# Layer 2 mixture of experts in a four-layer decoder: weighted rows scattered behind each expert, loaded in order, and the last expert's rows added by one product

## What is computed

```python
logits = xf @ Wr.T
topk_vals, topk_idx = jax.lax.top_k(logits, TOP_K)             # TOP_K = 2
w_flat = softmax(topk_vals).reshape(-1)
sort_idx = jnp.argsort(topk_idx.reshape(-1))                   # 1600 (token, expert) rows, sorted by expert
rev = sort_idx // TOP_K
chunks = xf[rev].reshape(Ne, S // Ne, Ds)                      # 200 rows for each expert, in order
h = gelu(einsum('ecd,edf->ecf', chunks, W1), approximate=False)
eo = einsum('ecf,efd->ecd', h, W2).reshape(S, Ds)
out = zeros((N, Ds)).at[rev].add(eo * w_flat[sort_idx][:, None])
```

## Time and profile before

| | us |
|---|---|
| three runs | 1495.36, 1498.70, 1505.01 |
| median | 1498.7 |
| the profiled execution's own time | 1495.78 |
| its span, first to last instruction | 1494.0 |
| PE busy, share of the span | 91% |
| granted TensorE clock, mean | 0.954 |

### The profile page before, as it was taken

How to read it: one execution, slowest core, us unless ns; L and a number is a source line. 1 busy time by engine, 2 the same in 40 slices (tenths; PEclk the granted TensorE clock), 3 DMA queues, 4 the chain that set the end, 5 groups by cost and what they waited for, 6 DMA issues and landing times. The chain is left out here.

```text
span 1494.0 us, 31527 instructions
## 1 busy us (share of the span) xinstructions
PE 1353.9 (91%) x12488; PEld 1054.5 (71%) x12488; DVE 769.4 (52%) x1733; ACT 646.7 (43%) x1683; POOL 194.9 (13%) x200
## 2 busy tenths in 40 slices
PE   7999899989989899899999889989957896899887
PEld 6776668866557588778999765669955675578632
DVE  3666677655556677520000477501127485566765
ACT  3444226633366366344444246432225674256300
POOL 3000250000024200050110420040042000300000
PEclk9999999989999999899999989989988997999999
DMA  6000331011301200366996100545211000700100
GB/s 217 1 1 1 68 65 22 4 44 43 80 8 21 46 11 4 130 210 244 343 342 261 49 22 1 227 166 202 74 52 40 1 2 1 118 5 4 68 1 22
DMA packets 43943, 120.19 MB, mean 80 GB/s; under 512 B 11931, under 2 KB 28440, under 8 KB 38412
## 3 DMA queue, kind: packets, MB, share of 16 engines
q1 hardware_dynamic: 33048, 62.04, 14.4%
q0 software_dynamic: 7616, 53.12, 10.3%
q10 hardware_dynamic: 3136, 3.03, 0.7%
HBM read 95.78 MB, written 11.00 MB: 71 GB/s over the span
## 5 line engine op out<-in xcount | busy, mean ns | idle before, releaser
L826 PE MATMUL wide<-early_kt,early_q 32*100 32x361 f32 x512 | 95.4, 485 | 2.8 <-PEq L66 1.6
L2555 ACT ACTIVATE l1f_hidden<-wide,l1f_pack 128x128 f32<-128x128 f32 x160 | 58.8, 368 | 78.0 <-PE wide L2494 68.1
L2677 DVE TENSOR_TENSOR l1f_out<-summed,l1f_pack 128x256 f32<-128x256 f32 x20 | 8.5, 425 | 152.8 <-PE summed L2502 152.8
L2494 PEld LDWEIGHTS wide<-l1f_rt,l1f_pack 128*128 128x128 f32 x640 | 74.5, 192 | 1.7 <-issue 0.8
L2494 PE MATMUL wide<-l1f_rt,l1f_pack 128*128 128x128 f32 x640 | 74.8, 275 | 0.6 <-ACT l1f_rt L2545 0.6
L113 PE MATMUL summed<-ident 128*128 128x128 f32 x302 | 44.4, 314 | 33.2 <-PEq L66 33.2
L2502 PE MATMUL summed<-l1f_pack,l1f_hidden 128*128 128x256 f32 x320 | 72.4, 379 | 0.0
L113 PEld LDWEIGHTS summed<-ident 128*128 128x128 f32 x302 | 42.2, 226 | 38.9 <-issue 38.9
L2502 PEld LDWEIGHTS summed<-l1f_pack,l1f_hidden 128*128 128x128 f32 x320 | 59.2, 190 | 7.2
L3688 PE MATMUL wide<-l3f_we,l3f_xt 128*100 128x512 f32 x128 | 59.6, 620 | 1.2 <-DVE l3f_acc L3756 1.2
L1220 DVE TENSOR_REDUCE l3x_mx<-wide 100x2 f32<-100x722 f32 x64 | 55.3, 904 | 3.2 <-PE wide L826 3.0
(11 more groups left out here) (605 smaller groups left out, 3369.8 us busy)
## 6 DMA issues: line engine op xcount, KB each, us to landing
l2f_w<-l2f_w_dram SPq DMA_DIRECT2D x16, 1024.0 KB, 11.5
ctxt<-ctxt_dram SPq DMA_DIRECT2D x4, 1083.0 KB, 17.1
early_kt<-soon_kd SPq DMA_DIRECT2D x32, 90.8 KB, 3.3
l1f_sorted_x<-l1f_zeros SPq DMA_DIRECT2D x4, 640.0 KB
l1f_rows<-l1f_sorted_x SPq DMA_DIRECT2D x20, 128.0 KB, 7.5
l1f_sorted_y<-l1f_out ACTq DMA_DIRECT2D x20, 128.0 KB, 9.4
l0f_w<-l0f_w_dram SPq DMA_DIRECT2D x18, 128.0 KB, 2.1
l1f_shared<-l1f_shared_dram SPq DMA_DIRECT2D x1, 2180.0 KB, 9.0
```

Source lines behind the costliest of these rows:

```text
L826: pe.matmul(wide[0:S, i, 0:SKV], q4[R * i:R * (i + 1), g % 2, b, g // 2, :], kt[R * i:R * (i + 1), g % 2, b, g // 2, 0:SKV], start=True, s ...
L2494: last = pe.matmul(wide[:, f % 4, 0:P], w1_of(w, k, f), rt[:, n % 2, k, :], start=k == 0, stop=k == KC - 1)
L2555: act.activation(hidden[:, f, 0:P], wide[:, f % 4, 0:P], ACT.Gelu, bias=b1_of(pack[:, n % SLOTS, :], f)).then_inc(sem["h_ready"], 1)
L2677: dve.tensor_tensor(out[:, n % 2], summed[:, n % 2, 0:E], b2_of(pack[:, n % SLOTS, :]), ALU.add).then_inc(sem["y_ready"], 1)
```

## The change

Rows now carry three more numbers (`ROW = E + 3`): the weight of the token for this expert, the slot in which the result is to lie, and the token's number. Two new inputs, `l2f_tags` and `l2f_numbers`, are loaded for it. `xn` holds two copies of the normalised tokens, one for each choice, and the weights are made early: ACT begins with the Exp table, takes the exponential ahead of the unit copies and then loads the Gelu table. Behind each of the experts 0 to 6, DVE scales `out` by the rows' weights and POOL scatters it to `token_y`, each row to its token's slot, with two indirect DMAs. Zeros are scattered to the slots of the last expert. SP then loads `token_y` in order, in four parts, and DVE adds them to x. The last expert's rows don't go through DRAM: `spot`, made of `numbers` on DVE, holds the weight where row and token meet, and PE multiplies it with `out` (`unsort`), in eight pieces that DVE adds to x. The units ahead of the experts are 28 (`AHEAD = 6`); `rest[0]` and `turn_out(6)` stand between the experts 6 and 7, and ACT makes the copies of expert 7. The statistics of layer 3's norm are taken at the end of `l2_ffn`, piece by piece behind the additions, and `keep_busy` in `l3_attn` goes from 18 to 4.

```diff
-    AHEAD = 4
+    AHEAD = 6
+    ROW = E + 3
+    PARTS = 4
+    FIN = NE - 1
...
+        tags, numbers = sb("tags", [S, TOP, B, 2]), sb("numbers", [S, B * S])
+        pairs = [(wr[:], dram["l2f_wr"]), (t.iota[:], dram["iota8"]), (before[:], dram["before"]), (tags[:], dram["l2f_tags"]),
+                 (numbers[:], dram["l2f_numbers"].partition_broadcast(S))]
         n_loaded = 16 * len(pairs)
-        xn = sb("xn", [S, B, E])
+        tokens = sb("tokens", [S, TOP * B * ROW])
+        xn = tokens[:].rearrange("s (k b e) -> s k b e", k=TOP, b=B)
+        back = tokens[:, 0:TOP * B * E].rearrange("s (n e) -> s n e", e=E)
...
+        rows = sb("rows", [S, SLOTS, RT, ROW])
+        about, target = sb("about", [S, NE, RT, 3]), sb("target", [S, NE * RT], U32)
+        spot = sb("spot", [S, RT, B * S])
+        none = sb("none", [S, E])
...
+        token_y = nc.dram_tensor("token_y", (ROWS, E), F32).ap()
...
                     if e + SLOTS < NE:
                         sp.wait_ge(sem["rt_psum"], e + 1)
+                        sp.wait_ge(sem["about_ready"], e + 1)
                         load_rows(e + SLOTS)
                         sp.wait_ge(sem["y_psum"], e + 1)
                         load_expert(e + SLOTS)
-                    sp.wait_ge(sem["y_ready"], e + 1)
-                    sp.dma_start(sorted_y.rearrange("(e r s) d -> e s r d", r=RT, s=S)[e], out[:, e % 2]).then_inc(stored[e % 2], 16)
+                sp.wait_ge(sem["none_stored"], 16 * RT)
+                for slot in range(2):
+                    sp.wait_ge(stored[slot], 16 * RT * ((FIN + 1 - slot) // 2))
+                for n in range(PARTS):
+                    some = slice(n * TOP * B // PARTS, (n + 1) * TOP * B // PARTS)
+                    sp.dma_start(back[:, some], token_y.rearrange("(n s) d -> s n d", s=S)[:, some]).then_inc(gathered[n], 16)
...
+                pool.memset(none[:], 0.0)
+                pool.drain()
                 pool.wait_ge(sem["place_ready"], 1)
                 for b in range(B):
                     for k in range(TOP):
                         pool.indirect_dma_start(out=sorted_x, out_offset=bass.IndirectOffsetOnAxis(ap=placei[:, k * B + b:k * B + b + 1], axis=0),
-                                                in_=xn[:, b, :], in_offset=None).then_inc(sem["scattered"], 16)
-                for slot in range(2):
-                    pool.wait_ge(stored[slot], 16 * NE // 2)
-                for b in range(B):
-                    for k in range(TOP):
-                        pool.indirect_dma_start(out=back[:, k * B + b, :], out_offset=None, in_=sorted_y,
-                                                in_offset=bass.IndirectOffsetOnAxis(ap=placei[:, k * B + b:k * B + b + 1], axis=0)
-                                                ).then_inc(gathered[k * B + b], 16)
+                                                in_=xn[:, k, b, :], in_offset=None).then_inc(sem["scattered"], 16)
+
+                def scatter(e, source, done):
+                    for c in range(RT):
+                        pool.indirect_dma_start(out=token_y, out_offset=bass.IndirectOffsetOnAxis(ap=target[:, e * RT + c:e * RT + c + 1], axis=0),
+                                                in_=source(c), in_offset=None).then_inc(done, 16)
+
+                for e in range(FIN):
+                    pool.wait_ge(sem["y_ready"], e + 1)
+                    scatter(e, lambda c: out[:, e % 2, c, :], stored[e % 2])
+                pool.wait_ge(sem["about_ready"], NE)
+                scatter(FIN, lambda c: none[:], sem["none_stored"])
...
+                def unsort(b):
+                    bank = (turned, summed)[b % 4 // 2][0:S, b % 2, b // 4 * E:(b // 4 + 1) * E]
+                    if b >= 4:
+                        pe.wait_ge(sem["added"], b - 3)
+                    for c in range(RT):
+                        last = pe.matmul(bank, spot[:, c, b * S:(b + 1) * S], out[:, FIN % 2, c, :], start=c == 0, stop=c == RT - 1)
+                    last.then_inc(sem["back_psum"], 1)
+
+                rest = order[2 * (B + AHEAD):]
...
+                        if e == FIN and f == unit[rest[0]] % RING:
+                            pe.wait_ge(unit_free[f], unit[rest[0]] // RING + 1)
                         for k in range(KC):
                             last = pe.matmul(wide[:, f % 4, 0:CR], w1[:, e % SLOTS, k, f * P:(f + 1) * P], rt[:, e % 2, k, :], start=k == 0, stop=k == KC - 1)
                         last.then_inc(sem["h_psum"], 1)
-                    if e >= 1:
+                    if 1 <= e < FIN:
                         turn_out(e - 1)
                     if e + 1 < NE:
                         turn(e + 1)
                     weigh(e)
-                rest = order[2 * (B + AHEAD):]
-                project(rest[0])
-                turn_out(NE - 1)
-                for what in rest[1:]:
+                    if e == FIN - 1:
+                        project(rest[0])
+                        turn_out(e)
+                project(rest[1])
+                turn_out(FIN)
+                project(rest[2])
+                pe.wait_ge(sem["spot_ready"], RT)
+                pe.wait_ge(sem["y_ready"], NE)
+                for b in range(B):
+                    unsort(b)
+                for what in rest[3:]:
                     project(what)
...
-                act.preload_act_table(ACT.Gelu)
+                act.preload_act_table(ACT.Exp)
...
+                act.wait_ge(sem["gap_ready"], 1)
+                act.activation(t.exp[:], t.gap[:], ACT.Exp).then_inc(sem["exp_ready"], 1)
+                act.preload_act_table(ACT.Gelu)
...
-                act.wait_ge(sem["gap_ready"], 1)
-                act.activation(t.exp[:], t.gap[:], ACT.Exp).then_inc(sem["exp_ready"], 1)
-                for what in order[2 * (B + AHEAD):]:
+                    if e == FIN - 1:
+                        copy_unit(rest[0])
+                act.wait_ge(sem["y_psum"], NE)
+                act.activation(yt[:, FIN % 2], summed[:, 0, 0:KC * CR].rearrange("p (m s) -> p m s", m=KC), ACT.Copy).then_inc(sem["yt_ready"], 1)
+                act.wait_ge(stored[FIN % 2], 16 * RT * (FIN // 2))
+                act.wait_ge(sem["o_psum"], NE)
+                act.activation(out[:, FIN % 2], summed[0:S, 1, :].rearrange("s (c e) -> s c e", c=RT), ACT.Copy).then_inc(sem["y_ready"], 1)
+                act.preload_act_table(ACT.Sqrt)
+                for what in rest[1:]:
                     copy_unit(what)
+                act.wait_ge(sem["var_ready"], 2)
+                act.activation(net.std[:], net.std[:], ACT.Sqrt).then_inc(sem["std_ready"], 1)
...
+                    normalise(dve, net, xn[:, 0, b, 0:E], b).then_inc(sem["xn_ready"], 1)
+                for b in range(B):
+                    normalise(dve, net, xn[:, 1, b, 0:E], b)
...
+                dve.tensor_copy(xn[:, :, :, E + 1:ROW], tags[:])
...
+                dve.wait_ge(sem["exp_ready"], 1)
+                dve.tensor_scalar(t.den[:], t.exp[:], 1.0, None, ALU.add)
+                dve.drain()
+                dve.reciprocal(xn[:, 0, :, E:E + 1], t.den[:])
+                dve.drain()
+                dve.tensor_tensor(xn[:, 1, :, E:E + 1], t.exp[:], xn[:, 0, :, E:E + 1], ALU.mult)
...
                 dve.tensor_copy(placei[:], place[:].rearrange("s k b -> s (k b)")).then_inc(sem["place_ready"], 1)
-                for e in range(NE):
+
+                def learn(e):
+                    dve.wait_ge(r_loaded[e % SLOTS], 16 * (e // SLOTS + 1))
+                    dve.tensor_copy(about[:, e], rows[:, e % SLOTS, :, E:ROW])
+                    dve.drain()
+                    dve.tensor_copy(target[:, e * RT:(e + 1) * RT].unsqueeze(2), about[:, e, :, 1:2]).then_inc(sem["about_ready"], 1)
+
+                for e in range(FIN):
+                    learn(e)
                     dve.wait_ge(sem["y_psum"], e + 1)
                     dve.tensor_copy(yt[:, e % 2], summed[:, 0, 0:KC * CR].rearrange("p (m s) -> p m s", m=KC)).then_inc(sem["yt_ready"], 1)
                     dve.wait_ge(sem["o_psum"], e + 1)
                     if e >= 2:
-                        dve.wait_ge(stored[e % 2], 16 * (e // 2))
-                    dve.tensor_copy(out[:, e % 2], summed[0:S, 1, :].rearrange("s (c e) -> s c e", c=RT)).then_inc(sem["y_ready"], 1)
-                dve.wait_ge(sem["exp_ready"], 1)
-                dve.tensor_scalar(t.den[:], t.exp[:], 1.0, None, ALU.add)
-                dve.drain()
-                dve.reciprocal(t.prob[0][:], t.den[:])
-                dve.drain()
-                dve.tensor_tensor(t.prob[1][:], t.exp[:], t.prob[0][:], ALU.mult)
-                dve.drain()
+                        dve.wait_ge(stored[e % 2], 16 * RT * (e // 2))
+                    for c in range(RT):
+                        last = dve.tensor_scalar(out[:, e % 2, c, :], summed[0:S, 1, c * E:(c + 1) * E], about[:, e, c, 0:1], None, ALU.mult)
+                    last.then_inc(sem["y_ready"], 1)
+                learn(FIN)
```

(34 more changed lines are left out.)

21 lines of the change are left out of this document (11 added, 10 removed).

## The result

Median of four runs 1481.86 us, beside 1501.86 for four runs of the kernel before on the same chip: ratio 0.988, 95% interval 0.985 to 0.9911. Timed once more on another occasion (six runs, eleven of before), it was 1485.46 against 1498.41, ratio 0.989 (0.9852 to 0.9928). The forecast was 1485.5, range 1479.5 to 1492. So the time is where it was forecast, and the gain, 1.1 to 1.2% by these ratios, is at the border of the case that I gave 0.76 ("within 1%"); the intervals reach to both sides of it. Single runs of after lie between 1476.49 and 1491.65 us, so a median within 4 us of the forecast is in part luck.

The account below looks back on a forecast made before the run. PE was busy 91% of the span, but the prediction read waits in the changed stage. -2.4 - 10.7 + 1.2 = -11.9 us gave 1483.9 on the profiled execution, 1486.8 on the median's scale; forecast 1485.5, range 1479.5 to 1492.

Parts of the forecast that it names:

- within 1%: Whole kernel: time differs from before by no more than about 15 us either way; chance 0.76.
- Front, -2.4: Routing to first expert: four more value units keep PE busy until rows land, expert 0 at full clock; net -2.4 us.
- the one on the new loads: Front: two new loads delay SP's others some 0.4 us each, but PE needs them only after the first transposes.
- Loop, nothing: Experts' loop: POOL's scatters, SP's added wait and DVE's scalings fit beside PE's period of over 11 us; no change.
- End, -10.7: Last expert to next block: ordered loads and a product replace gathers; the next block starts 10.7 us earlier.
- Rival 1: End of feed forward gives gain back through PE's clock, spot or slow loads; sum -5 to -10 us; chance 0.22.
- Its second part: End of feed forward: building spot on DVE holds up POOL's scatters, +2.1 us.
- Rival 3: Scatters of 1036-byte rows cost POOL more each; a doubling gives +8.7 us, 1504.5; chance 0.05.
- Layer 3's attention, +1.2: Its start: memset holds the norm, keys may run at half clock; first reduction at 14.3 us instead of 13.09.
- Rival 2: Layer 3's attention: norm precedes memset, clock up at keys, reduction near 10.1 to 11; sum -15 to -16.5 us; chance 0.15.
- Sum: Whole kernel: -2.4 - 10.7 + 1.2 = -11.9 us on the profiled execution's 1495.78, giving 1483.9.

Follow-up runs that it names:

- e1: Kernel after with four value units ahead of the first expert instead of eight; feed forward block 170.95 us against 164.25.
- e7: Kernel before with eight value units ahead of the first expert instead of four, nothing else; feed forward block 173.45 us against 176.50.
- before_again: Kernel before, unchanged, profiled once more for the spread; feed forward block 175.04 us, layer 3's attention 153.93 us.
- after_again: Kernel after, unchanged, run once more for the spread; median 1485.46 us, ratio to before 0.989; feed forward block 163.59 us.
- e6: Kernel after with 26 idle products ending PE's feed forward and 28 instead of 8 starting layer 3's attention; blocks 170.09 and 145.15 us.
- e3: Kernel after with POOL's memset of l3a_v issued behind the norm of layer 3's attention; that block 146.03 us against 147.11.
- e8: Kernel after with late numbers and tags, memset behind norm, PE's pauses filled, exponential of beta behind ACT's first two copies; median 1479.44 us, ratio to before 0.9862.
- e2: Kernel after with tags and numbers loaded behind the value weights under their own semaphore; feed forward block 162.50 us against 164.25.

## Why the prediction was right, and where not

*Front, -2.4.* The mechanism is shown by e1 and e7: with the four units PE's clock stays up and expert 0's second product starts 1.5 to 3 us earlier. From the first scatter to that product it is 35.68 us in before, 34.12 in before_again, and 32.98 in after. But in the profile after only 0.8 of the gain was left at the mark itself (57.82 against 58.62), in after_again 2.9. The step that failed is the one on the new loads, "PE needs them only after the first transposes": PE waited 0.98 us in the midst of them. The key units then began 1.04 us later than in before and their first 16 instructions took 1.12 longer at half clock, which isn't shown to come from the loads; the first scatter came 1.9 us later. The numbers were issued 1.55 us after the block's start and took 4.6 us from issue to PE's use; I had not set their landing against the logits, only their issue. The sentence behind it, that a late load would shift the whole front, was right.

*Loop, nothing.* From the start of expert 0's second product to the end of expert 6's it is 75.25 us in before and in after.

*End, -10.7.* Measured -11.45 (from the end of expert 6's second product, 1084.33 in after, to the next block: 42.64 before, 31.19 after). From that end on, forecast and measured: scaling done 3.15 and 3.24, last scatter started 7.3 and 7.39, loads issued 10.0 and 10.08, last part added 21.5 and 21.8, reciprocal done 30.1 and 30.1, next block 32.0 and 31.19. Two terms were off and small: the parts came 1.77 to 2.17 us apart, not 1.7, and the barrier took 1.07, not 1.89. The chain was right in every step: each wait was put down to a row that measured the same chain before (last scatter to load, load to landing). That it came out so closely is in part luck. From the issue of the loads to the last addition it took 11.70 us in after, the shortest of the nine profiles with these loads and the product; the others go up to 13.53, with a mean of 12.5, where the forecast had 11.5. And in after the clock stayed up; in after_again the end gained 10.0 us.

*Rival 1.* Its clock is real: PE's clock fell in the pause before the fifth product in five of seven profiles of kernels with this end, and not in after. Where `bn_stats` stands between the additions it cost 0.3 to 0.4 us in three and 1.8 in one (e6), not 2.1. Its second part didn't happen: `spot` lay beside two scatters, and these kept 0.98 us with 0.30 between them. By the rule of the Trainium skill, "SBUF — State Buffer", section "Who interferes with whom", descriptor writing should have been shut out; no run here shows that. For the memset the same rule is borne out by e3, with 2.67 us against 5.45.

*Rival 3.* It didn't happen: the 16 scatters of longer rows took 0.98 us each, as in before.

*Layer 3's attention, +1.2.* Measured: the first reduction came 0.2 us earlier than in before (12.95 against 13.14) and 1.1 later than in before_again in the worse run (13.53 against 12.42), so between -0.2 and +1.1. Over the six profiles that begin as after does its mean is 13.6, over before, before_again and e7 12.8: +0.8. Either way the 4.25 us of statistics brought nothing here, as forecast. The memset held the norm (it ended at 5.51, forecast 5.8) and the keys ran at half clock as feared. The term that was mis-sized is the way from norm to keys: I had put transposes and copies behind the norm's end, but they begin as soon as the first groups are there, and the keys began at 7.61 instead of 8.85. Rival 2, that DVE's norm comes ahead of the memset, happened in no run that left the memset at the start; where edits put the norm first, kept the clock up and took the loads of `beta` out of ACT's way (e8), the reduction came at 8.11, below its 10.1 to 11.

*Sum.* Forecast -11.9. In the two first profiles the three places give -0.8 - 11.45 - 0.2 = -12.45, so the errors of +1.6, -0.75 and -1.4 cancel in part, and that is luck. By means of two profiles each they give -1.1 - 10.8 + 0.5 = -11.4. The two whole blocks give -13.3 between the two first profiles and -12 to -15 between the means, and both timings -13 to -20 by medians. The medians' excess over the blocks is not explained: the untouched blocks vary by 13 us from one execution to the next, and no run shows that the change moves them.

## To carry to other kernels

Here the chain that ends a stage was forecast to about a microsecond by taking each of its waits from a row of the same kind of wait before. A load that a change adds has to be set against the first use of whatever is behind it or shares its semaphore. Before crediting work that is taken off the start of a stage, look at what else runs there and had been hidden by it: here a memset and the clock gave back the 4.25 us, and moving the memset, ACT's wait for a load and the clock's fall out of the way (e8) brought the first reduction 5 us forward. What is pushed to a stage's end has to be followed through every queue: four units more behind the products cost 4.3 us through ACT, not through PE.

## What the hardware showed

- Before the fifth product of `unsort`, PE pauses of 2.07 us (after) and 2.93 us (e3) left the clock at 1.00, pauses of 2.16 (e2) and 2.36 us (e1) at the same place were followed by 0.50: the pause alone doesn't decide it. In this order:

```profile
1106.68 1.97 PE L3051 MATMUL turned<-l2f_out,l2f_spot 100*100 100x256 f32 x8 [2.07 <-DVE x L3230]
1113.86 1.97 PE L3051 MATMUL turned<-l2f_out,l2f_spot 100*100 100x256 f32 x8 [2.93 <-DVE x L3230]
1102.91 2.37 PE L3052 MATMUL turned<-l2f_out,l2f_spot 100*100 100x256 f32 x8 [2.16 <-DVE x L3232]
1107.39 3.27 PE L3051 MATMUL turned<-l2f_out,l2f_spot 100*100 100x256 f32 x8 [2.36 <-DVE x L3230]
```

- Two DVE instructions on 800 columns took 0.65 us each (after), quicker than the 1.05 estimated from the norm, and did not hold POOL's indirect DMAs beside them.
- An indirect DMA of 100 rows took 0.98 us of POOL and 0.30 between two, for rows of 1024 (before) and 1036 bytes (after) alike.
- A product of 128 x 128 in float32 ran as two instructions (52 for 26 in e6); a count of idle products is half the count of instructions.
